# Softmax attention: VectorE instead of GpSimd normalises every second unit's probabilities in place

## The reference

```
q, k, v = norm(x) @ w_q, norm(x) @ w_k, norm(x) @ w_v
scores  = q @ k.T + bias[head]            # 256 x 256
prob    = softmax(scores)                 # exp(s - max), divided by its row sum
context = prob @ v
x       = x + concat(context of 16 heads) @ w_o
```

## Time and profile before

| | |
|---|---|
| median of three runs | 2808.46 us |
| profiled execution, own time | 2834.32 us |
| its span | 2832.5 us |
| busy, share of the span: TensorE, VectorE, ScalarE, GpSimd | 71%, 74%, 57%, 62% |
| softmax attention, from the first L2119 to the last | about 1606 us to 2588 us of the span |
| L2307 over the whole span | 512 instructions, mean 581 ns, 291.6 us |
| L2124 over the whole span | 512 instructions, mean 626 ns, 300.5 us |

### The profile page before, as it was taken

One profiled execution on the slowest core, in us unless ns is written; L12 is line 12 of the kernel. 1 busy time (PEld: TensorE's weight loads), 2 busy tenths in 40 slices (PEclk: granted clock), 3 DMA queues, 4 the chain that ended last, 5 costly groups with the idle time before them and its releaser, 6 DMA issues. The chain is left out here.

```text
span 2832.5 us, 62063 instructions
## 1 busy us (share of the span) xinstructions
PE 2017.6 (71%) x15531; PEld 1499.7 (53%) x15531; DVE 2083.9 (74%) x8002; ACT 1607.1 (57%) x4581; POOL 1754.5 (62%) x2414
## 2 busy tenths in 40 slices
PE   2225888658332578860588699999999999996887
PEld 2224777546322477760366455665555656554565
DVE  4423787778442377785899888889898988886897
ACT  3213444345321344434455589889889988885564
POOL 4554566600455455662456488888888888885565
PEclk9999999879555799985799899999999999997999
DMA  5114333240211433326000166666666666664000
GB/s 172 38 44 113 109 107 107 78 126 0 111 38 43 116 106 101 106 84 187 34 0 0 35 137 139 141 143 140 145 141 141 142 144 139 145 141 94 12 22 26
DMA packets 703409, 272.37 MB, mean 96 GB/s; under 512 B 560020, under 2 KB 688852, under 8 KB 702468
## 3 DMA queue, kind: packets, MB, share of 16 engines
q1 hardware_dynamic: 680628, 229.75, 33.8%
q0 software_dynamic: 17408, 35.82, 4.0%
q10 hardware_dynamic: 5200, 4.84, 0.5%
HBM read 59.31 MB, written 44.24 MB: 37 GB/s over the span
## 5 line engine op out<-in xcount | busy, mean ns | idle before, releaser
L2218 ACT ACTIVATE p_prob<-p_neg,p_neg_max 128x256 f32<-128x256 f32 x1024 | 508.2, 503 | 1.6 <-DVE p_neg_max L2113 1.6
L1044 POOL DMA_INDIRECT results_by_token<-p_e_result,p_e_slot x288 | 284.9, 989 | 255.0 <-DVE p_e_result L987 178.3
L2113 DVE CUSTOM_DVE_ANT_0 p_neg<-p_s_ps,top_bias 128x256 f32<-128x256 f32 x1024 | 384.9, 412 | 50.0 <-PE p_s_ps L2396 44.3
L730 POOL DMA_INDIRECT rows_by_expert<-p_r_z,p_r_target x256 | 247.1, 965 | 201.7 <-issue 112.0
L881 PE MATMUL p_e_o_ps<-p_w,p_e_hT 128*128 x2304 | 297.3, 282 | 11.2 <-issue 10.3
L918 ACT ACTIVATE p_e_hT<-p_e_h_ps,p_b 128x256 f32<-128x256 f32 x576 | 230.1, 476 | 128.7 <-remote 63.8
L2124 DVE SCALAR_TENSOR_TENSOR p_parts<-p_prob,p_scaled_inverse,p_parts 128x256 f16<-128x256 f32 x512 | 300.5, 626 | 0.7 <-POOL p_parts L2298 0.7
L2314 POOL TENSOR_TENSOR p_parts<-p_prob,p_parts 128x512 f16<-128x512 f32 x256 | 296.4, 1158 | 0.0
L2307 POOL TENSOR_SCALAR p_prob<-p_prob,p_inverse 128x256 f32<-128x256 f32 x512 | 291.6, 581 | 5.2 <-DVE p_inverse L2119 3.5
L2396 PE MATMUL p_s_ps<-p_qkT 64*128 64x256 f32 x2048 | 290.7, 403 | 0.8 <-ACT p_qkT L2236 0.7
L881 PEld LDWEIGHTS p_e_o_ps<-p_w,p_e_hT 128*128 128x128 f32 x2304 | 281.0, 198 | 19.3 <-issue 16.6
(11 more groups left out here) (270 smaller groups left out, 5142.2 us busy)
## 6 DMA issues: line engine op xcount, KB each, us to landing
p_e_z<-rows_by_expert SPq DMA_DIRECT2D x144, 129.0 KB
p_e_affine<-p_affine SPq DMA_DIRECT2D x144, 128.0 KB
p_got<-results_by_token SPq DMA_DIRECT2D x64, 256.0 KB, 2.9
p_e_b<-p_b SPq DMA_DIRECT2D x144, 64.0 KB
p_probT<-p_parts SPq DMA_TRANSPOSE x512, 2.8
results_by_token<-p_e_result,p_e_slot POOLq DMA_INDIRECT x288
p_r_w<-in_w SPq DMA_DIRECT2D x2, 2048.0 KB, 8.4
p_w<-in_w SPq DMA_DIRECT2D x2, 2048.0 KB, 11.8
```

The costliest lines, as they stand in the source:

```text
L730: pool.indirect_dma_start(dram_rows, bass.IndirectOffsetOnAxis(ap=target[s][:, r, k:k + 1], axis=0), z[s][:, r, k, :], None).then_inc(scat ...
L1044: pool.indirect_dma_start(dram_results, bass.IndirectOffsetOnAxis(ap=slot[q][:, t:t + 1], axis=0), result[q % 2][:, t, :], None).then_inc( ...
L2113: ins = v.tensor_tensor_reduce(neg[k % NEGS][:, t, :], s_ps[k % SCORES][:, t, :], bias[:, t, h, :], -1.0, HUGE, ALU.add, ALU.min, neg_max[ ...
L2218: ins = act.activation(prob[k % PROBS][:, t, :], neg[k % NEGS][:, t, :], ACT.Exp, bias=neg_max[k % NEGS][:, t:t + 1], scale=-1.0, accum_ou ...
```

## The change

`normalise` goes from GpSimd's stream to VectorE's. It has the same two `tensor_scalar` instructions per odd unit, in place on the float32 prob, and the same two semaphores. In VectorE's iteration k (k odd) it stands behind `biased_max` of unit k+3 and the projection's instruction, and ahead of `low_part` of unit k-1 and `invert` of unit k+1. GpSimd's loop keeps `high_part` of unit k+1 and `low_part` of unit k-2. The semaphore `taken` is no longer raised for odd units.

```
+            def normalise(i, k):                          # in VectorE's block
+                v.wait_ge(inverse_ready, i * GROUP_UNITS + (k + 1))
+                for t in range(SEQ_TILES):
+                    ins = v.tensor_scalar(prob[k % PROBS][:, t, :], prob[k % PROBS][:, t, :], inverse[k % PROBS][:, t:t + 1],
+                                          PROB_SCALE, ALU.mult, ALU.mult)
+                ins.then_inc(normalised, 1)
...
+                    if split_by(k) == BY_POOL:             # VectorE's body
+                        normalise(i, k)
                     if k > 0 and split_by(k - 1) == BY_VECTOR:
                         low_part(i, k - 1)
...
-            def normalise(i, k):                          # in GpSimd's block
-
-                pool.wait_ge(inverse_ready, i * GROUP_UNITS + (k + 1))
-                pool.sem_inc(taken, 1)
-                for t in range(SEQ_TILES):
-                    ins = pool.tensor_scalar(prob[k % PROBS][:, t, :], prob[k % PROBS][:, t, :], inverse[k % PROBS][:, t:t + 1],
-                                             PROB_SCALE, ALU.mult, ALU.mult)
-                ins.then_inc(normalised, 1)
...
                 for k in range(1, GROUP_UNITS, 2):        # GpSimd's body
-                    (high_part if split_by(k) == BY_VECTOR else normalise)(i, k)
-                    if k + 1 < GROUP_UNITS or ahead:
-                        behind = unit_behind(i, k, 1)
-                        (high_part if split_by(behind[1]) == BY_VECTOR else normalise)(*behind)
+                    if split_by(k) == BY_VECTOR:
+                        high_part(i, k)
+                    if (k + 1 < GROUP_UNITS or ahead) and split_by(k + 1) == BY_VECTOR:
+                        high_part(*unit_behind(i, k, 1))
```

## The result

The changed kernel takes 2844.61 us (median of four runs, 2839.05 to 2848.8) against 2808.44 us before (2802.5 to 2812.57): +36 us. The ratio is 1.0121, with a 95% interval of 1.0096 to 1.0147, that is 27 to 41 us. The forecast was 2830 (2798 to 2858), slower with a chance of 0.70. The profiled execution took 2839.05 us, only 5 above that of before, but that compares other phases too, which the change doesn't touch: the span outside this layer is 1850 us in the profile before and 1828 after. Within the layer, from the first L2119 to the last, the two profiles have 982.3 and 1008.9 us: +26.6.

The account below looks back on a forecast made before the run. It took the reciprocal–GpSimd–transposition–TensorE loop and VectorE/GpSimd exclusion as the bounds. A 3.80 us pair floor plus once-a-group VectorE work gave 3.91 us a pair, +0.085 x 256 = +22 us on 2808.46: 2830 us, range 2798 to 2858.

Parts of the forecast that it names:

- What bounds the kernel: Loop of reciprocal, GpSimd, transposition, TensorE, maxima and low_part, three pairs long; GpSimd no backlog; tight pairs 3.50 us, mean 3.825.
- Price of the instruction: VectorE's moved TENSOR_SCALAR of 128x256: 0.35 us undisturbed, 0.26 to the next start, 0.52 us a pair.
- The wait: On VectorE, the first normalise of a pair is held 0.4 us until GpSimd's low_part (L2314) ends.
- The floor: Shortest pair, even reciprocal to even reciprocal on VectorE: rises from 3.50 to 3.80 us, none shorter.
- a sign of being wrong: In the changed profile: pairs under 3.8 us, or the new instruction taking 0.2 us or not held up.
- The sum: Over 256 pairs: 3.91 us a pair, +0.085 each, +22 us; lower end -6, upper end +90 us.
- VectorE's work once a group: L160, L2151 and L2134 on VectorE: 2.26 us, about half hidden, 1.1 to 2.3 us a group added.
- Hidden: Rival, 15%: VectorE's net added 0.2 us a pair fits in its 0.38 us of waits; 2808 us.
- faster: Rival, 15%: GpSimd off the shared access frees VectorE's L2124, reciprocals come earlier, TensorE's waits halve; -28 us, 2780 us.
- one element a step: Rival, 22% together with nearly all additive: VectorE's normalise at 0.39 us each, no lock; +47 us, 2856 us.
- Nearly all additive: Rival, 22% together with one element a step: half of VectorE's additive end, 0.18 us a pair; +46 us, 2856 us.
- GpSimd's wait: Sign: GpSimd's wait for VectorE's reciprocal rises from 0.46 to some 1.5 us a pair.

Follow-up runs that it names:

- no_norm: Changed kernel with VectorE's normalise left out, odd units undivided, ScalarE's high_part waiting for the reciprocal: 2800 us, ratio to before 0.9982.
- norm_last: Changed kernel with normalise moved behind the reciprocal of unit k+1 in VectorE's iteration: 2811 us, ratio to before 1.0022.
- only_seventh: Changed kernel with normalise only where k % 8 = 7, left out in the other odd units: 2834 us, ratio to before 1.0116.
- before_low_first: Kernel before with GpSimd's low_part of unit k-2 put ahead of high_part of unit k+1: 2768 us, ratio to before 0.9866.
- unlocked: Changed kernel with each tensor_scalar of normalise replaced by a one-input tensor_reduce of 128x184 that GpSimd doesn't hold up: 2844 us, ratio to before 1.0130.
- half_norm: Changed kernel with only the first of normalise's two tensor_scalar, second half of odd units undivided: 2819 us, ratio to before 1.0051.
- after_low_first: Changed kernel with GpSimd's low_part of unit k-2 put ahead of high_part of unit k+1: 2917 us, ratio to before 1.0435.
- low_first_swapped: after_low_first with low_part ahead of normalise in VectorE's iteration: 2951 us, ratio to before 1.0497.
- low_first_unlocked: low_first_swapped with each tensor_scalar of normalise replaced by a tensor_reduce of 128x184: 2773 us, ratio to before 0.9842.

## Why the prediction was right, and where its reason was not

*What bounds the kernel.* Right in its first half: the loop from the reciprocal over GpSimd, the transposition and TensorE sets the pair, and GpSimd has no backlog. no_norm shows the second, norm_last, only_seventh and before_low_first the first. It was not followed up: the prediction took the loop as three pairs long, over scores and maxima, and never asked which VectorE iteration it passes. It is four pairs long, over a projection, ScalarE and `keep_low_second`.

*Price of the instruction.* Forecast 0.35 us undisturbed; measured 345 ns (minimum 339, median 345), two in 0.60. `low_part` forecast at 474 to 475; measured 474. Where the first `normalise` of a pair starts inside L2314, in 163 of 256 pairs, it ends 0.147 us (median) after it; forecast 0.15. Over 0.5 us, as forecast for every pair, it takes in 131 of the 256 pairs. The wait, forecast at 0.4 us, comes to 0.17 us a pair on average.

*The floor.* Forecast 3.80 us; the usual shortest pair is 3.75 to 3.76 us, 84 of 255. But 95 of 255 are under 3.8, which the prediction had named as a sign of being wrong, and 5 are under 3.75, down to 3.39. This was the step that failed: the prediction said that the sum follows from this floor because short pairs can't make up for long ones any more. unlocked took the floor down to 3.39 us and the group stayed at 62.8. The short pairs had slack; when they shorten, VectorE waits for scores.

*The sum.* Forecast +0.085 us a pair as the nearer of two bounds, 22 us; measured 0.108 in the stretch, 26.6 us over the layer, 36 (27 to 41) in total. In its place stands: `normalise` delays the reciprocal by 0.52 us once in four pairs on the loop, 2.1 us a group (60.8 to 62.9), and the quieter `low_part` gives 0.3 back. That is 1.8 x 16 = 29 us. The rest, up to the 36 us of the runs, lies within the interval and has no experiment. That the forecast of 22 came near was luck: it was added up from a floor and from VectorE's work once a group, and the floor is worth at most 2 us. No run tests the work once a group.

*The rivals.* "Hidden" and "faster" are out by the measured time, and one element a step by the 0.26 us from one `normalise` to the next. The relief that the faster rival counted on is real (0.31 us a pair on VectorE) but worth 5 us, as VectorE wasn't the limit. "Nearly all additive" is out by half_norm, where a quarter of the work arrives. GpSimd's wait, forecast at 1.5 us a pair, was 1.69; TensorE's share, forecast 92%, was 91%. VectorE's waits came to about 24 us, under the 40 forecast.

## What to carry to other kernels

A wait or an instruction costs what it delays on the loop that closes last. Find in which iteration the loop passes the engine, and put off-loop work behind the instruction that releases the others: here, behind the reciprocal, the same work costs a quarter (0.5 instead of 2.1 us a group). Engines at 90% each may still be limited by a chain of waits; the gain was in the order of GpSimd's stream (1.3%), not in who does the work, and the same reorder in the changed kernel cost 4.3%. Before shifting an instruction that shares an access with another engine, look at who starts that other engine's instruction: if it is, through a third engine, the delayed one, the delay can repeat in every round, as it did here.

## What the runs showed of the hardware

- A float32 TENSOR_SCALAR of 128x256 from SBUF in place with a scalar per partition takes 345 ns on VectorE, 0.26 us to the next start; a TENSOR_REDUCE of 128x184 takes 335 to 337 ns.
- The TENSOR_SCALAR and a SCALAR_TENSOR_TENSOR with two SBUF inputs wait for GpSimd's TENSOR_TENSOR: one `low_part` takes up to 1435 ns in after_low_first. Of 256 elements, the held TENSOR_SCALAR ends 0.15 us after GpSimd's instruction, the held `low_part` 0.28 us; GpSimd's instruction waits for theirs (1369 ns on average in low_first_swapped instead of 1158). The TENSOR_REDUCE, with one input, ran beside GpSimd's instruction undisturbed (at most 351 ns in low_first_unlocked, where 156 of 512 start inside L2314).
- A shared access that costs at most 2 us in one order of the streams cost 178 us in another, which had not been expected.
